# A graph layer pair on one core: node work moved from between and behind two edge phases into their loops

## The reference

```python
hi = x[src] @ w1;  hj = x[dst] @ w2
e = leaky_relu(hi + hj, 0.3) * a                      # logits: sums over 16 channels, 8 heads
attn = softmax of the logits over the edges of each destination
x = layernorm(x + segment_sum(hi * attn, dst))

ef = (relu(attr @ We1 + be1) @ We2 + be2) * sigmoid(ew @ Wt + bt)
msg = relu(concat([x[src], ef]) @ Wn1 + bn1) @ Wn2 + bn2
x = layernorm(x + (segment_sum(msg, dst) + x))
```

## Time and profile before

| | |
|---|---|
| median of 3 runs | 2329.46 us (2328.28 to 2330.48) |
| the profiled execution | 2327.27 us |
| its span, first to last instruction | 2325.5 us |
| PE busy | 2007.7 us (86%) |
| POOL busy | 1610.2 us (69%) |
| DVE busy | 1235.8 us (53%) |
| ACT busy | 663.7 us (29%) |
| granted TensorE clock, mean | 0.92 |

### The profile page before, as it was taken

One profiled execution on the slowest core, in us unless ns is written; L12 is line 12 of the kernel. 1 busy time (PEld: TensorE's weight loads), 2 busy tenths in 40 slices (PEclk: granted clock), 3 DMA queues, 4 the chain that ended last, 5 costly groups with the idle time before them and its releaser, 6 DMA issues.

```text
span 2325.5 us, 45201 instructions
## 1 busy us (share of the span) xinstructions
PE 2007.7 (86%) x12672; PEld 1317.7 (57%) x12673; DVE 1235.8 (53%) x2842; ACT 663.7 (29%) x1433; POOL 1610.2 (69%) x1692
## 2 busy tenths in 40 slices
PE   6589888899898898898778889988998989898884
PEld 5366666665666665666555555555555555555553
DVE  5455555555555555555465555555555555555555
ACT  5111111111111111111143333434343434334344
POOL 4677777777777777777006777777777777777771
PEclk9698989997989988989778999999999999999997
DMA  7532232223322223232125554545545455545442
GB/s 193 140 82 84 83 82 83 80 78 83 83 83 82 76 82 82 83 82 64 31 74 150 127 133 128 132 128 132 132 128 133 127 133 127 132 128 132 129 114 67
DMA packets 251926, 245.45 MB, mean 106 GB/s; under 512 B 143119, under 2 KB 189200, under 8 KB 251886
## 3 DMA queue, kind: packets, MB, share of 16 engines
q1 hardware_dynamic: 197214, 134.38, 21.1%
q0 software_dynamic: 53648, 109.59, 18.9%
q10 hardware_dynamic: 1024, 0.98, 0.2%
HBM read 229.77 MB, written 10.27 MB: 103 GB/s over the span
## 4 chain that ended last, share of the span: by engine, by line
PE 34%; POOL 27%; issue 23%; DVE 7%; DVEq 2%; DMA 2%; ACT 1%; POOLq 1%; SPq 0%; ACTq 0%
POOL T L605 26%; PE ps L1354 9%; PE ps L1346 7%; PE ps L1339 7%; PE ps L1389 5%; PE ps L1393 3%; DVEq L1002 2%; DVE R L1053 1%; DVE E L995 1%; ACT V L720 1%; POOL G L572 1%; DVE XM L1057 1%; DMA T<-in_x 1%; DVE st L1075 1%; PE ps L1413 1%
## 5 line engine op out<-in xcount | busy, mean ns | idle before, releaser
L605 POOL DMA_INDIRECT T<-y_rows,idx x832 | 793.9, 954 | 373.3 <-issue 370.6
L572 POOL DMA_INDIRECT G<-hi_rows,idx x832 | 806.0, 969 | 282.9 <-issue 262.5
L1486 PE MATMUL ps<-G 128*128 128x64 f32 x1664 | 229.2, 281 | 101.8 <-ACT G L794 99.3
L1339 PE MATMUL ps<-ident,G 128*128 128x128 f32 x832 | 204.2, 333 | 126.9 <-DVE XM L1057 45.9
L794 ACT ACTIVATE G<-G 128x512 f32<-128x512 f32 x208 | 131.0, 630 | 616.0 <-DVE G L1180 616.0
L995 DVE TENSOR_TENSOR E<-ps,V 128x512 f32<-128x512 f32 x208 | 142.6, 686 | 287.7 <-ACT V L720 286.7
L1486 PEld LDWEIGHTS ps<-G 128*128 128x128 f32 x1664 | 203.3, 192 | 151.2 <-ACT G L794 122.4
L1180 DVE TENSOR_TENSOR G<-ps,T 128x512 f32<-128x512 f32 x208 | 143.8, 691 | 261.8 <-DMA T<-y_rows,idx 259.8
L720 ACT ACTIVATE V<-ps 128x512 f32<-128x512 f32 x208 | 124.3, 598 | 545.7 <-PE ps L1346 544.3
L1354 PE MATMUL ps<-E,AwP 128*32 128x128 f32 x1940 | 252.7, 302 | 10.4 <-DVE E L995 10.3
L1339 PEld LDWEIGHTS ps<-ident,G 128*128 128x128 f32 x832 | 117.0, 160 | 217.2 <-issue 215.1
(11 more groups left out here) (147 smaller groups left out, 2231.7 us busy)
## 6 DMA issues: line engine op xcount, KB each, us to landing
T<-in_edge_weight SPq DMA_DIRECT2D x207, 256.0 KB, 3.5
Dbc<-block_destinations SPq DMA_DIRECT2D x69, 384.0 KB, 3.6
T<-in_edge_attr SPq DMA_DIRECT2D x207, 128.0 KB, 2.4
G<-hi_rows,idx POOLq DMA_INDIRECT x832, 2.6
T<-y_rows,idx POOLq DMA_INDIRECT x832
T<-in_x SPq DMA_DIRECT2D x12, 448.0 KB, 6.8
link<-scan_destinations SPq DMA_DIRECT2D x70, 56.4 KB
y_rows<-T SPq DMA_DIRECT2D x7, 448.0 KB, 3.2
```

What stands on the lines that cost most here:

```text
L572: pool.indirect_dma_start(out=G[:, s, t * C:(t + 1) * C], out_offset=None, in_=hi_d[:, :], in_offset=bass.IndirectOffsetOnAxis(ap=idx[:, s ...
L605: pool.indirect_dma_start(out=Yb[:, r, t * C:(t + 1) * C], out_offset=None, in_=y_d[:, :], in_offset=bass.IndirectOffsetOnAxis(ap=idx[:, r ...
L1339: pe.matmul(U[j][:, i * P:(i + 1) * P], G[:, s, t * C:(t + 1) * C], ident[:, :], is_transpose=True, start=(i == 0), stop=False, skip_group ...
L1486: ins = pe.matmul(ps[4][:, 0:W], hS[:, i * C:(i + 1) * C], ohB[:, i * W:(i + 1) * W], start=(i == 0), stop=(i == 3))
```

## The change

Three blocks of nodes are taken per turn of four steps of the first phase (MB = 3, MC = 15 turns, MLAG = 3 turns behind the step's own count), and the last MN = 4 blocks after the loop. In step 0 of a turn ScalarE copies a strip of `acc` out (`mT`, `mD`), PE transposes it, and VectorE does `attention` and later `moments_of`; in step 1 ScalarE clears the strip and VectorE computes the inverse root and scales (`normal`); in step 2 PE transposes the result and ScalarE copies it; in step 3 PE multiplies it and VectorE adds the bias. SP loads x, keeps the normalised rows in a table in memory (`x1_d`, since `T` is still in use) and stores y. After the loop all of `X1` is loaded back.

In the second phase, from turn LAG = 7 on, one block per turn is multiplied by Wn2, summed, normalised and stored (LOOPED = 46 blocks); three remain for the tail. The square root is replaced by an integer guess and three Newton steps on VectorE, eleven dependent instructions (`inverse_root`), in both places. `E` and `V` become one tensor, so ScalarE waits for the logits before it writes. The flag is also raised if the edge list would let an addition come to a block after its turn. The old code of the middle and the tail moves into the slow path.

```diff
-        E = sb("E", [P, GQ, QE])
+        E = V
...
+            with eng.Fori(lag - 1, turns) as k:
+                for i in range(RG):
+                    step(RG * k + RG + i, i, k + 1, k + 1 - lag)
...
+            with eng.Fori(LAG, NQ // RB - 1) as k:
+                for r in range(RB):
+                    edge(k * RB + r, r, k, k - LAG)
...
@@ SP, first phase @@
+                    if s == 0:
+                        keep_rows(m)
+                    if s == 2:
+                        load_rows(m + 1)
+                    if s == 3:
+                        store_rows(m)
...
+                run_steps(sp, step, MLAG + 1)
+                keep_rows(MC - 1)
+                store_rows(MC - 1)
...
+                sp.wait_ge(s_u, NQ)
+                sp.wait_ge(s_n["kept"], 16 * MC)
+                sp.dma_start(X1[:, 0:MC * MB, :], x1_d.rearrange("(b p) c -> p b c", p=P)).then_inc(s_n["back"], 16)
+                sp.wait_ge(s_n["ys"], MC + 1)
+                sp.dma_start(y_d[b0:NB * P, :].rearrange("(b p) c -> p b c", p=P), yE).then_inc(s_n["stored"], 16)
...
@@ POOL, before the second phase @@
+                pool.wait_ge(s_n["stored"], 16 * (MC + 1))
...
@@ ACT, first phase @@
-                        need(act, s_lk, (f - 1) * GQ + j + 1)
+                        need(act, s_log, (f - 1) * GQ + j + 1)
...
+                    if nodes and s == 0:
+
+                        act.wait_ge(s_acc, 2 * GQ * (g - 3))
+                        need(act, s_n["y"], m)
+                        need(act, s_n["t"], m)
+                        passed(act, "act")
+                        cut = bass.ds(m * (MB * P), MB * P)
+                        act.activation(mT[:, :], accH[:, cut], ACT.Copy)
+                        act.activation(mD[:, :], accD[:, cut], ACT.Copy).then_inc(s_n["copy"], 1)
                     scaled(0)
+                    if nodes and s == 1:
...
+                        act.activation(accH[:, bass.ds(m * (MB * P), MB * P)], AwP[:, 0:1].to_broadcast([P, MB * P]),
+                                       ACT.Copy).then_inc(s_n["zero"], 1)
...
                     scaled(1)
+                    if nodes and s == 2:
+                        act.wait_ge(s_n["xT"], m + 1)
+                        act.activation(mT[:, :], AG[1][:, 0:MB * P], ACT.Copy).then_inc(s_n["xTc"], 1)
                     scaled(2)
...
@@ DVE, first phase: ahead of leaky(2), and at the end of a step @@
+                    if nodes and s == 0:
+                        dve.wait_ge(s_n["t"], m + 1)
+                        dve.wait_ge(s_n["x"], 16 * (m + 1))
+                        attention(m, MB, AG[1], AG[1][:, MB * C:MB * C + MB * DC], count[:, bass.ds(m * MB, MB)],
+                                  mXb, mX[:, :])
+                    if nodes and s == 3:
+                        dve.wait_ge(s_n["y"], m + 1)
+                        need(dve, s_n["stored"], 16 * m)
+                        dve.tensor_tensor(mYb, AG[1][:, 0:MB * C].rearrange("p (b c) -> p b c", b=MB),
+                                          bn1B[:, :].unsqueeze(1).to_broadcast([P, MB, C]), ALU.add).then_inc(s_n["ys"], 1)
                     leaky(2)
...
+                    if nodes and s == 0:
+                        moments_of(m, MB, mXb)
+                    if nodes and s == 1:
+                        dve.wait_ge(s_n["mv"], m + 1)
+                        inverse_root(MB, s_n, m)
+                        normal(m, MB, mXb, mXb)
...
+                seen(dve.tensor_scalar(v, mv[:, 0, 0:n, 1], EPS, None, ALU.add))
+                seen(dve.tensor_scalar(t.bitcast(I32), v.bitcast(I32), 1, None, ALU.arith_shift_right))
+                seen(dve.tensor_scalar(y.bitcast(I32), t.bitcast(I32), -1.0, float(0x5f3759df), ALU.mult, ALU.add))
+                for i in range(3):
+                    seen(dve.tensor_tensor(t, y, y, ALU.mult))
+                    seen(dve.scalar_tensor_tensor(out=t, in0=t, scalar=-0.5, in1=v, op0=ALU.mult, op1=ALU.mult))
+                    ins = dve.scalar_tensor_tensor(out=y, in0=t, scalar=1.5, in1=y, op0=ALU.add, op1=ALU.mult)
+                    if i < 2:
+                        seen(ins)
...
@@ PE, first phase: between sums(1) and logits(f, s, 0), and ahead of aggregate(1) @@
+                    if nodes and s != 1:
+
+                        pe.wait_ge(s_acc, 2 * (GQ * (p - 1) + 2))
+                    if nodes and s == 0:
+                        pe.wait_ge(s_n["copy"], m + 1)
+                        for i in range(MB):
+                            pe.transpose(AG[1][:, i * C:(i + 1) * C], mT[:, i * P:(i + 1) * P], ident[:, :])
+                            ins = pe.transpose(AG[1][:, MB * C + i * DC:MB * C + (i + 1) * DC], mD[:, i * P:(i + 1) * P],
+                                               ident[0:DC, 0:DC])
+                        ins.then_inc(s_n["t"], 1)
+                    if nodes and s == 2:
+                        pe.wait_ge(s_n["x1"], m + 1)
+                        for i in range(MB):
+                            ins = pe.transpose(AG[1][:, i * P:(i + 1) * P], mXb[:, i, :], ident[:, :])
+                        ins.then_inc(s_n["xT"], 1)
+                    if nodes and s == 3:
+                        pe.wait_ge(s_n["xTc"], m + 1)
+                        for i in range(MB):
+                            ins = pe.matmul(AG[1][:, i * C:(i + 1) * C], mT[:, i * P:(i + 1) * P], wN1[:, 0, :],
+                                            start=True, stop=True)
+                        ins.then_inc(s_n["y"], 1)
                     logits(f, s, 0)
...
                     logits(f, s, 1)
+                    if nodes and s != 1:
+                        pe.wait_ge(s_n[("xs", None, "xTc", "ys")[s]], m + 1)
                     aggregate(1)
...
@@ second phase: ACT at the end of r == 0, PE at the end of r == 1, DVE at the end of r == 2 and r == 3 @@
+                        act.activation(aF, accH[:, bass.ds(m * P, P)], ACT.Copy).then_inc(s_f["copy"], 1)
...
+                        pe.matmul(ps[5][:, 0:C], aF, wN2[:, :], start=True, stop=True).then_inc(s_f["o"], 1)
...
+                        if r == 2:
+                            dve.wait_ge(s_x2, m + 1)
+                            finish(m, 1, ps[5][:, 0:C], X1[:, bass.ds(m, 1), :].rearrange("p b c -> p (b c)"), xF, yF)
+                        if r == 3:
+                            scale(m, 1)
+                            need(dve, s_out[0], 16 * m)
+                            normalise(m, 1, xF, yF)
```

More of the change, by code:

```diff
@@ L423, in _ @@
[L423 to L429, removed]
+                    if is_int(g) and g == 2:
+                        load_rows(0)
+                    if m is None:
+                        return
+                    if s == 0:
+                        keep_rows(m)
@@ L776, in _ @@
                     act.activation(hR, zR, ACT.Relu).then_inc(s_3["h"], 1)
+                for c in range(NC):
+                    deviation(c, s_f)
+                    need(act, s_out[c % 2], 16 * (c // 2))
+                    scale_rows(c, s_f, xs[c % 2], yS[c % 2])
             with act.Else():
@@ L1006, in add @@
                         dve.tensor_tensor(w_, AG[j % 2][0:DC, W:2 * W], w_, ALU.add).then_inc(s_acc, 1)
+                    nodes = m is not None and (not is_int(m) or m < MC)
                     def nxt(j):
@@ new lines, in _ @@
+                attention(MC, MN, ps[0], ps[3][:, 0:MN * DC], count[:, MC * MB:NB], xE, V[:, 0, :])
+                moments_of(MC, MN, xE)
+                dve.wait_ge(s_n["mv"], MC + 1)
+                inverse_root(MN, s_n, MC)
+                normal(MC, MN, xE, X1[:, MC * MB:NB, :])
+                dve.memset(accH[:, MC * MB * P:NP], 0.0)
+                dve.wait_ge(s_n["y"], MC + 1)
+                dve.tensor_tensor(yE, ps[2][:, 0:MN * C].rearrange("p (b c) -> p b c", b=MN),
+                                  bn1B[:, :].unsqueeze(1).to_broadcast([P, MN, C]), ALU.add).then_inc(s_n["ys"], 1)
@@ L1131, in add_shares @@
+                dve.wait_ge(s_n["zero"], MC)
+                dve.wait_ge(s_n["back"], 16)
+                dve.wait_ge(s_n["x1"], MC + 1)
             def add_shares(b):
@@ L1477, in _, with edge @@
                 pe.wait_ge(s_3["back"], NB + 1)
+                for c in range(NC):
+                    need(pe, s_f["xs"], c - 1)
+                    for i in range(NCH):
+                        n0 = (c * NCH + i) * P
+                        ins = pe.matmul(bank(2 * (c % 2), i), accH[:, n0:n0 + P], wN2[:, :], start=True, stop=True)
+                    ins.then_inc(s_f["o"], 1)
             with pe.Else():
-                def edge(q, r, k):
+                def edge(q, r, k, m):
                     g4, z, e, h, t = (later(q, lag) for lag in (4, 3, 2, 1, 0))
```

483 lines of the change are left out of this document (322 added, 161 removed).

## The result

The changed kernel takes 2342.6 us (median of 9 runs, 2337.4 to 2354.7) where the kernel before takes 2326.6 (9 runs, 2319.1 to 2330.5): a ratio of 1.0085, 95% interval 1.0065 to 1.0105. It is slower, by 0.85%, where I forecast 2.2% faster. The profiled execution took 2350.5 us, with a span of 2348.7 and a granted clock of 0.887.

A forecast was written before the change was run, and what follows sets the result against it. Gathers and PE were taken to bound the first phase side by side, gathers the second. Terms -62 - 27.5 + 34 + 3 = -52.5 gave 2277 us, 2.2% faster; range 2244 to 2318, the forecast's own 2258 to 2297.

The forecast's parts named there:

- Middle: Between the phases: four blocks remain, first y gather 19 us after the last addition; -62 us, bounds -58 to -66.
- Tail: After the second phase's last addition: 12.1 us remain of 39.7; -27.5 us, bounds -25 to -29.
- First phase: PE's added node work, 14 turns x 2.5, less 5 slack, plus 4 in the drain: +34 us, bounds 4 to 75.
- rival 1: First phase: gathers stay the bound as the clock settles at full level; phase +4, 2247 us; chance 0.17.
- POOL's waits for msg: First phase, expected profile sign: these waits rise from 20 us to some 50, as gathers then wait for PE.
- Second phase: Node work added to the loop hides in slack; only stretched gathers cost: +3 us, bounds 0 and +16.
- The 0.7: Second phase: a delay of 0.7 us after group 3, made up in the next two groups, costing nothing.
- Rival 4: Second phase: the chain falls behind the gathers by VectorE's 2.8 us; 0.35 per turn, +13, 2290 us; chance 0.05.
- 1.28 or more: Second phase: gather stream forecast at 1.26 us each; a stream this slow would prove the prediction wrong.
- stretched gathers: Second phase: more VectorE operations beside POOL's gathers may lengthen them; +3 us, the phase's only cost in the sum.
- Prologue: Before the flag: eight small VectorE steps of 0.2 us fall in a 3 us idle and cost nothing.
- Rival 3: First phase: VectorE's node work lands on PE's chain, 6.3 us per turn exposed; 94 more, 2371 us; chance 0.10.

The follow-up runs named there:

- first part: Changed kernel with the last product and norm back behind the second phase's loop, leaving only the first phase's node work: 2271.1 us, ratio 0.977.
- spread: Changed kernel with the second phase's norm cut into four pieces over the turn, scaled and stored one turn later: 2243.2 us, ratio 0.966.
- second-phase filler: Changed kernel with six unread PE products per turn ahead of PE's wait for ScalarE in the second phase: 2250.2 us, ratio 0.967.
- one iteration: Changed kernel with one iteration of the root instead of three in the second phase and tail: 2243.5 us, ratio 0.965.
- early judgement: Spread-root kernel with seven small VectorE steps judging block order moved ahead of VectorE's wait for PE in the prologue: 2246.2 us, ratio 0.965.
- first-phase filler: Spread-root kernel with two more unused PE products per first-phase step, ahead of PE's wait for XM: 2242.4 us, ratio 0.963.
- 12 dry steps: Kernel before with 12 dependent VectorE steps computing nothing after every fourth second-phase group: median 2411.2 us, ratio 1.037; runs left out 2371.3 and 2402.8.
- 8 steps: Kernel before with 8 dependent VectorE steps computing nothing after every fourth group of the second phase: 2335.0 us, ratio 1.003.
- 15 steps: Kernel before with 15 dependent VectorE steps computing nothing after every fourth group of the second phase: 2424.9 us, ratio 1.043.

## Why the prediction was wrong

**Middle, right.** Forecast 19 us from the last addition to the first y gather, -62; measured 18.4 and -62.9.

**Tail, right.** Forecast 12.1 and -27.5; measured 11.4 and -28.3.

**First phase, the term mis-sized.** Forecast +34; the changed kernel shows +6.8. Over the five traces with the old first phase it is 1039.7 us on average (1036.0 to 1043.5), over the six with the node work done once and no filler in this phase (changed, first part, spread, second-phase filler, one iteration, early judgement) 1044.9 (1041.9 to 1049.0): +5, near the +4 of my first rival. I had foreseen POOL's waits for msg to rise from 20 to 50 us; they fell to one wait of 15.2 us at the start, and rose to 42.7 in 27 waits only with the node work done twice. The working took PE's 2.5 us per turn as added to a path with 5 us of slack. How busy PE became can be read from the early-judgement kernel, which has the same node work in this phase and whose records are whole. First its window, then that of the first-phase filler:

```profile
112.73:1161.69 1048.96, 945.91 (x7168) 659.14 (x7166) 640.73 (x1702) 183.37 (x462) 761.53 (x784) 0.91 0.31 85
112.21:1152.89 1040.68, 954.39 (x7398) 681.19 (x7397) 639.61 (x1702) 183.90 (x462) 759.85 (x784) 0.97 0.32 86
```

PE's busy time rose by 20.4 us, from 925.5 to 945.9, and not by 35, with the clock up from 0.90 to 0.91, and its idle time fell from 112.5 to 103.1. So a part of the new work was paid for in clock and a part stands where PE would have waited. Two more products per step, some 30 us at full clock, added 8.5 us of busy time at a clock of 0.97, left 86.3 idle, and were free as well. And POOL, which never waited for msg but once at the start, kept the pace: the growth of 5 us lies in the stream of gathers (1.282 us each on average over the six traces, 1.275 over the five) and not behind its last one; what stretched it by so little was not looked into. There is an end to it: the same node work once more, at the same places, costs all of its 38 us. Whether that is for its place or for coming in bursts of 1.2 us was not told apart.

The Trainium skill (TensorE: Matmul & The Clock Gate, Part 4, PE-mode transpose) says that transposes do not count as PE-busy in the same way; nine of the twelve new operations per turn are transposes, and by that only the three products could have raised the clock. The traces show it at 0.91 to 0.92 with the node work and at 0.89 to 0.90 without, and at 0.97 with products as filler. They can't separate the three products from the nine transposes, so the rule is neither shown nor refuted here.

**Second phase, the step that failed.** "VectorE waits 1.3 us per group for rows, 5 per turn against the 3.3 added [...] A delay of 0.7 after group 3 is made up in the next two. Nothing by that." The chain is 3.0 us, near the 2.8 forecast, and the slack is there. Three things were wrong:
- The slack was summed over a turn. A chain in one piece meets only the slack of its own group, and 0.6 to 1.06 us of issue before L1414, which used to lie inside VectorE's idle time, come on top. The 0.7 has no working in the prediction; 2.8 less the 1.3 of one group would have been 1.5. PE's wait at this place is 2.2 us, where its waits were 0.64 on average, 1.6 more.
- Even that wait is made up, as I had it: 19.5 us is under 20.2. But I let the delay end with the wait, and put the clock at nothing. PE's clock falls behind it, and the slow products take 3.1 us more per turn: this is the cost that was missing.
- Rival 4 had this place and VectorE's delay, priced at 0.35 us per turn, and not the clock. It is 2.3 per turn (104 us over 46).

Against the spread kernel, which does the same work: PE busy 1045.4 against 955.1 us, 90 more from slower products alone; PE idle 114.3 against 100.4, 14 more.

I forecast "the second gather stream at 1.26 us each" and named 1.28 or more as the sign of being wrong: it is 1.37 (832 gathers, the first at 1177.6 and the last at 2317.4). The 3 us of the sum for stretched gathers are 0: 791.0 us of gathers against 793.9. The Trainium skill (SBUF — State Buffer, Who interferes with whom) says that a VectorE operation with two SBUF inputs locks GpSimd's reads out for its length; from it I had estimated up to 12 us for the root. The same section of the Trainium skill takes the writing of a transfer's descriptors by GpSimd to be free of this, as an inference. The traces fit that: in the spread kernel, where all of the root stands in the loop, the gathers took 794.3 us (793.9 before) and the phase did not grow.

**Prologue.** Forecast 0, measured +3.75 in this trace. The first waiting gather comes at 111.2 on average (110.1 to 113.2) in the five traces with the old prologue and at 113.9 (112.2 to 115.9) in the seven with the new one, the two with early judgement (112.7 and 114.0) not among them: some 2.7 us of it seems to be the change's, though the two ranges overlap. The order of the judging steps isn't shown to be the cause, and the cause stays open.

**The rivals.** The gathers stayed the bound of the first phase, as rival 1 had it, but not for its reason, since the clock is 0.92 there and not at the full level. Rival 3, the one that was to end slower, did not happen: in the whole first phase PE waits for VectorE's node work twice, 5.0 us in all, and 4.8 of them are the drain's, for which I had 4.

```profile
PE ps L1685 <- DVE mX L1315: 5.0, 2, 4.8
```

The kernel is slower at the place that I had at 0.05, at more than six times its price, and by a loss of clock that no rival named there.

## What to carry to other kernels

Slack summed over a turn covers work that is spread over the turn; a dependent chain in one piece has to fit into the slack of the place where it stands. Where PE is the busy engine, price a new wait twice: its length, and the products behind it at half speed. Waits of 0.6 us in two groups of three left the clock at 0.98 here; one of 2.2 us in every fourth group, with about the same sum, took it to 0.88 and cost 90 us of slower products. If such a wait can't be split, products that nobody reads may be cheaper than idling.

## What the runs showed of the hardware

- One wait of 2.2 us in some 22 us of otherwise dense products took the second phase's granted clock from 0.98 to 0.88; 135 waits of 0.64 us with about the same sum left it at 0.98. With dry steps on VectorE, 129 waits, nearly all of 1.2 us or less, left it at 0.98, one of 1.75 us per turn gave 0.90, and one of 2.3 us gave 0.88. The Trainium skill (TensorE: Matmul & The Clock Gate, Part 1, "A second HAM failure mode") tells of short idles between groups of products that make the clock swing between its two levels; the trace agrees, and here the length of the single wait told, not the sum.
- Adding 120 us of products (46 turns of 2.6) shortened the kernel by 92 us, with the second phase's clock at 1.00 instead of 0.88.
- With 12 dry steps the two runs that count lie 31 us apart, where seven with 8 steps range over 11 us and four with 15 steps over 8.
- The same kernel took 2327 us on one chip and 3317 on another; no trace here says why.
